# Five units' u times B: turned u scaled by columns of turned B on ScalarE, in place of products with diagonal matrices read back from DRAM

## What is computed

```python
dbc = jnp.einsum('bld,ed->ble', xi, x_proj)
dt, Bm, Cm = jnp.split(dbc, [DT_RANK, DT_RANK + D_STATE], axis=-1)
dt = jax.nn.softplus(jnp.einsum('blr,dr->bld', dt, dt_w) + dt_b)
A = -jnp.exp(A_log)
dA = jnp.exp(dt[..., None] * A)
dBx = (dt * xi)[..., None] * Bm[:, :, None, :]
def step(h, inp):
    a, bx, c = inp
    h = a * h + bx
    return (h, jnp.einsum('bds,bs->bd', h, c))
```

## Time and profile before

| | us |
|---|---|
| median of 3 runs | 4762.65 (4761.55 to 4768.12) |
| span of the profiled execution | 4760.7 |
| PE busy | 4479.5 (94%) |
| DVE busy | 3894.2 (82%) |
| ACT busy | 3109.7 (65%) |
| POOL busy | 3320.9 (70%) |

### The profile page before, as it was taken

How to read it: one execution, slowest core, us unless ns; L and a number is a source line. 1 busy time by engine, 2 the same in 40 slices (tenths; PEclk the granted TensorE clock), 3 DMA queues, 4 the chain that set the end, 5 groups by cost and what they waited for, 6 DMA issues and landing times. The chain is left out here.

```text
span 4760.7 us, 67108 instructions
## 1 busy us (share of the span) xinstructions
PE 4479.5 (94%) x24932; PEld 3395.1 (71%) x24932; DVE 3894.2 (82%) x4126; ACT 3109.7 (65%) x5158; POOL 3320.9 (70%) x1559
## 2 busy tenths in 40 slices
PE   7999999999999989999999999998799999999999
PEld 3666666666666666667666667666688888888888
DVE  5999999999999999999999999999854444444452
ACT  6777777777777777777777777777444444444443
POOL 4999999999999999999999999999820000000000
PEclk9999999999999999999999999999999999999999
DMA  7544444444444444444444444444231111010100
GB/s 271 178 142 141 134 151 132 136 134 134 143 139 134 155 132 138 129 139 139 131 147 140 129 130 136 143 142 156 103 123 32 36 32 36 32 36 32 36 23 10
DMA packets 297736, 545.76 MB, mean 115 GB/s; under 512 B 101888, under 2 KB 186624, under 8 KB 262784
## 3 DMA queue, kind: packets, MB, share of 16 engines
q1 hardware_dynamic: 296512, 529.91, 35.6%
q10 hardware_dynamic: 896, 11.54, 0.7%
HBM read 502.77 MB, written 50.14 MB: 116 GB/s over the span
## 5 line engine op out<-in xcount | busy, mean ns | idle before, releaser
L1400 DVE TENSOR_TENSOR_SCAN m_h<-bank,m_state,m_dBx 128x512 f32<-128x512 f32 x1512 | 1841.2, 1265 | 35.0 <-ACT bank L1145 27.2
L868 PEld LDWEIGHTS bank<-ident,m_h 128*128 128x128 f32 x8192 | 980.9, 143 | 417.2 <-issue 345.8
L868 PE MATMUL bank<-ident,m_h 128*128 128x128 f32 x8192 | 1197.6, 276 | 12.9 <-DVE m_h L1408 12.8
L1283 POOL TENSOR_TENSOR m_dBx<-u,m_Bs 128x1024 f32<-128x1024 f32 x432 | 1016.4, 2377 | 0.4 <-DMA m_Bs<-b_dram 0.2
L1283 POOL TENSOR_TENSOR m_dBx<-m_u,m_Bs 128x1024 f32<-128x1024 f32 x432 | 1015.5, 2371 | 1.2 <-DMA m_Bs<-b_dram 1.0
L1294 POOL TENSOR_TENSOR m_h<-m_h,m_Cs 128x1024 f32<-128x1024 f32 x384 | 909.4, 2368 | 105.8 <-ACT m_state L1077 105.1
L1408 DVE TENSOR_TENSOR m_h<-m_h,bank 128x1024 f32<-128x1024 f32 x640 | 767.0, 1198 | 51.7 <-PE bank L850 51.4
L1145 ACT ACTIVATE bank<-m_dt,cols 128x512 f32<-128x512 f32 x864 | 584.8, 688 | 225.2 <-DVE m_h L1400 223.7
L1145 ACT ACTIVATE bank<-dt,cols 128x512 f32<-128x512 f32 x864 | 584.1, 688 | 193.6 <-DVE m_h L1400 191.6
L302 POOL TENSOR_TENSOR mvj<-mvj,norm_c 128x4 f32<-128x4 f32 x16 | 16.5, 1032 | 969.0 <-DVE mvj L263 969.0
L731 PE MATMUL bank<-hT,w_in 128*128 128x512 f32 x1024 | 547.4, 630 | 113.1 <-ACT hT L998 105.8
(11 more groups left out here) (177 smaller groups left out, 5847.1 us busy)
## 6 DMA issues: line engine op xcount, KB each, us to landing
m_Bs<-b_dram SPq DMA_DIRECT2D x256, 1024.0 KB, 6.3
m_Cs<-c_dram SPq DMA_DIRECT2D x384, 256.0 KB, 3.7
m_dg<-d_dram SPq DMA_DIRECT2D x160, 256.0 KB, 3.9
xx<-in_x SPq DMA_DIRECT2D x16, 512.0 KB, 4.9
xn_dram<-xx SPq DMA_DIRECT2D x16, 512.0 KB, 4.5
yb_dram<-m_ysb SPq DMA_DIRECT2D x16, 512.0 KB, 5.0
xx<-xn_dram SPq DMA_DIRECT2D x16, 512.0 KB, 3.8
x_dram<-m_ysb SPq DMA_DIRECT2D x16, 512.0 KB, 5.0
```

The costliest lines, as they stand in the source:

```text
L868: mm = pe.matmul(YB[b][:, o:o + P], h[:, k % NH, m, tok:tok + P], ident[:, :], start=(s == 0 and o == 0), stop=False, is_transpose=True, s ...
L1283: pool.tensor_tensor(dBx[:, dbx_ring(ch, k) % NDBX, :, :], u[ch.batch][:, m, :], Bs[:, k // BP % 2, k % BP, :].unsqueeze(1).broadcast_to(( ...
L1400: dve.tensor_tensor_scan(o, decays, share, initial, ALU.mult, ALU.add).then_inc(S["scan"], 1)
```

## The change

The diagonal matrices go, with `d_dram`, its zeroing, the four writes per chunk, the loads and their semaphores. In their place a tile `m_uB` (same size as the two buffers of `m_dg`) holds the turned u scaled for one unit: on ScalarE `scale_u` multiplies each of the four token tiles (128 tokens x 256 channels) of `m_uT` by column k % 16 of the turned B, a scale per partition. The four activations of unit k stand at steps 2k - 5, 2k - 4, 2k - 3 and 2k - 2, behind the decay of the step. The first one waits until both fills of the five-unit list's previous unit are done (`a_fill`), since there is one `m_uB`. TensorE then turns `m_uB` into the bank with the identity, in transpose mode. ScalarE's copies of dt, B, C and of the turned u lose their waits for the diagonals' writes and the last fills.

```diff
-A_FIRST, A_STEP, NA = 19, 3, 5
-A_UNITS = tuple(A_FIRST + A_STEP * i for i in range(NA))
+A_UNITS = (19, 22, 25, 28, 31)
+NA = len(A_UNITS)
 B_UNITS = tuple(k for k in range(NU) if k not in A_UNITS)
-NBU, NDG, DIAG = len(B_UNITS), 2, T + 1
+NBU = len(B_UNITS)
+AT_US = (-5, -4, -3, -2)
...
-        dg = sb("dg", [P, NDG, TS, P])
+        uB = sb("uB", [P, TS, HW])
...
-            def store_diagonals(ch):
-
-                wait_drained(sp, ch, J_B)
-                if ch.first():
-                    sp.sem_inc(S["go"], 1)
-                    sp.wait_ge(S["d_init"], 16 * BATCH * NA)
...
-                sp.dma_start(dg[:, n % NDG, :, :], d_dram[ch.batch, i, 0:P * T].rearrange("(p t c) -> p t c", t=TS, c=P)
-                             ).then_inc(d_in[n % NDG], 16)
...
                     if m == 0:
-                        if i == 0:
-                            wait_drained(pe, ch, J_UT[1])
-                        pe.wait_ge(d_in[n % NDG], 16 * (n // NDG) + 16)
+                        pe.wait_ge(S["u_scaled"], n + 1)
                     pe.wait_ge(S["scan"], tile - NDA + 1)
                     for s in range(TS):
-                        mm = pe.matmul(DA[tile % NDA][:, s * P:(s + 1) * P], uT[:, s, m * P:(m + 1) * P],
-                                       dg[:, n % NDG, s, :], start=True, stop=True)
+                        mm = pe.transpose(DA[tile % NDA][:, s * P:(s + 1) * P], uB[:, s, m * P:(m + 1) * P], ident[:, :])
                     mm.then_inc(S["a_fill"], 1)
...
-                    if not ch.first():
-                        act.sem_inc(S["go"], 1)
-                        act.wait_ge(S["d_st"], ch.at(64, 0))
...
+            def scale_u(ch, g):
+
+                for i, k in enumerate(A_UNITS):
+                    for t in range(TS):
+                        if g != 2 * k + AT_US[t]:
+                            continue
+                        n = ch.at(NA, i)
+                        if t == 0:
+                            if i == 0:
+                                wait_drained(act, ch, J_UT[0])
+                                act.sem_inc(S["go"], 1)
+                                wait_drained(act, ch, J_UT[1])
+                                act.sem_inc(S["go"], 1)
+                                wait_drained(act, ch, J_C)
+                                act.sem_inc(S["go"], 1)
+                            wait(act, S["a_fill"], 2 * n)
+                        ins = act.activation(uB[:, t, :], uT[:, t, :], ACT.Copy,
+                                             scale=Ct[:, ch.batch, t, k % DS:k % DS + 1])
+                        if t == TS - 1:
+                            ins.then_inc(S["u_scaled"], 1)
...
+                    scale_u(ch, k)
```

More of the change, by code:

```diff
@@ L186, in adaln_mamba_ffn @@
         J = Join(S, x1, base, jx, jy, xn2, gain, norm_c, stat2, mvj, mv2)
-        d_dram = nc.dram_tensor("d_dram", (BATCH, NA, P * DIAG), F32, kind="Internal").ap()
         c_dram = nc.dram_tensor("c_dram", (BATCH, DS, T), F32, kind="Internal").ap()
         mamba(nc, a, bank, ident, cols, mod, gain, norm_c, fcol, any_odd, passes, w1, w2, J, x_v, yb_v, yf_v, xn_v, b_dram,
-              c_dram, d_dram, w_raw, S)
+              c_dram, w_raw, S)
         ffn(nc, a, sem, sbuf, bank, ident, mod, gain, fcol, any_odd, w1, w2, hT2, ot, J, w_raw, S, x_v, xn_v, yb_v, yf_v, out_v)
@@ L199 @@
     "sp_exp", "sp_ln", "dt_done", "u_ready", "b_st", "b_in0", "b_in1", "c_in0", "c_in1", "da", "dbx", "scan", "save",
-    "c_fill", "d_zero", "d_init", "d_st", "d_in0", "d_in1", "a_fill", "weigh_d", "weigh_p", "turned", "skip", "y_turned", "y_evac",
+    "c_fill", "u_scaled", "a_fill", "weigh_d", "weigh_p", "turned", "skip", "y_turned", "y_evac",
     "y_out", "xn_in", "xn_out",
@@ L356, in mamba @@
 def mamba(nc, a, bank, ident, cols, mod, gain, norm_c, fcol, any_odd, passes, w1, w2, J, x_v, yb_v, yf_v, xn_v, b_dram,
-          c_dram, d_dram, w_raw, S):
+          c_dram, w_raw, S):
     FB, DA, CB, YB = bank[0:2], bank[2:5], bank[5], bank[6:8]
     fill, drain = [S[f"fill{i}"] for i in range(NFB)], [S[f"drain{i}"] for i in range(NFB)]
-    b_in, c_in, d_in = (S["b_in0"], S["b_in1"]), (S["c_in0"], S["c_in1"]), (S["d_in0"], S["d_in1"])
+    b_in, c_in = (S["b_in0"], S["b_in1"]), (S["c_in0"], S["c_in1"])
     PASS = ("b_", "f_")
@@ L588, in load_c @@
                              ).then_inc(c_in[i % 2], 16)
-            def load_d(ch, i):
-                n = ch.at(NA, i)
-                wait(sp, S["a_fill"], 2 * (n - NDG + 1))
-                if i == 0:
-                    sp.sem_inc(S["go"], 1)
-                    sp.wait_ge(S["d_st"], ch.at(64, 64))
-                sp.dma_start(dg[:, n % NDG, :, :], d_dram[ch.batch, i, 0:P * T].rearrange("(p t c) -> p t c", t=TS, c=P)
-                             ).then_inc(d_in[n % NDG], 16)
             def store_y(ch):
@@ L628, in prologue @@
                 sp.dma_start(fcol[:, :, :], a["ffn_cols"]).then_inc(S["lng_in"], 16)
[L629 to L633, removed]
                 for n in range(6, 10):
@@ L638, in prologue @@
                 store_b(ch)
-                store_diagonals(ch)
                 for j in range(2):
@@ L675, in body @@
                 load_c(ch, 1)
-                load_d(ch, 0)
-                load_d(ch, 1)
                 if has(ch, 2):
@@ L696, in body @@
                     store_b(ch.go(1))
-                load_d(ch, 2)
                 load_c(ch, 8)
                 load_c(ch, 9)
-                load_d(ch, 3)
                 load_b(ch, 7)
@@ L705, in body @@
                 load_c(ch, 11)
-                load_d(ch, 4)
                 if has(ch, 1):
-                    store_diagonals(ch.go(1))
                     load_b(ch.go(1), 0)
@@ L1151, in keep_uT @@
                         wait_filled(act, ch, J_UT[m])
-                        wait(act, S["a_fill"], ch.at(2 * NA, 0))
                         b = BANK[J_UT[m]]
@@ L1330, in prologue @@
                 pool.memset(norm_c[:, 2, :], -1.0).then_inc(S["const"], 1)
-                pool.memset(dg[:, 0, :, :], 0.0).then_inc(S["d_zero"], 1)
                 pool.wait_ge(S["const"], 4)
```

1 line of the change is left out of this document (removed).

## The result

The changed kernel takes 4803.4 us (median of 4 runs, 4800.67 to 4805.4), the kernel before 4762.98 in the runs beside it: ratio 1.0082, 95% interval 1.0067 to 1.0096. It is slower, 40 us by the medians, against +49 forecast. The profiled execution's span is 4798.9 us, 38.2 above that of before.

The account below looks back on a forecast made before the run. VectorE bounds the kernel, its feeders just early enough. Per chunk +1.76 + 0.15 − 0.46 = +1.45 us, over 31 chunks +45, clock +4, on span 4760.7 gives 4810, median 4812 us; range 4764 to 4850.

Parts of the forecast that it names:

- The scaling's price: ScalarE's 20 new activations per chunk: 0.50 us each, 0.40 us of ACT time after overlap (0.28 to 0.49).
- The wait at step 51: ScalarE's step-51 scaling waits for unit 25's second fill, which waits for scan 48; the table load comes 1.22 us later.
- R3: Rival: the wait at step 51 does not bite, only the scalings' work; net 1.03 us a chunk, 4795 + 4; chance 0.13.
- DVE's stop: Late decays stop VectorE 1.56 us at scan 53, 1.76 us in all by scan 57, per chunk.
- Steps 33 to 37: Scalings at steps 33 and 34 delay ScalarE's copy of dt, B, C; VectorE's weighing comes 0.15 us later per chunk.
- Step 45: Shorter TensorE fills remove VectorE's wait for the spreading of C: −0.46 us a chunk (bounds nothing to −1.66).
- The clock: TensorE half-clock stretches at chunk starts, some 1.2 us each; four more chunks with one: +4 us.
- R1: Rival: TensorE's clock falls once more in every chunk, 37 in place of 4 us: 4845 us; chance 0.17.
- DMAs: Loads and writes of diagonals and the prologue's zeroing go; no engine waits for them: 0 taken, prologue 7 us at most.
- R2: Rival: TensorE is the real limit, shorter fills remove all waits for spreading (−51 us): 4712 to about 4740 us; chance 0.11.
- R4: Rival: VectorE's stop is given back as waits at the chunk's start shrink; 0.25 us a chunk, 4770 us; chance 0.09.

Follow-up runs that it names:

- The run with two buffers: The change with a second buffer for the scaled u of units 22 and 28, so no scaling waits for the previous unit's fills: 4770.1 us, ratio 1.0028.
- the filler: Unread identity transposes, 20 per chunk at step 1, added to the kernel with moved scalings: 4697.5 us; as ten identity products instead: 4698.6 us.
- the kernel before with filler: The kernel before the change plus 20 unread identity transposes per chunk on TensorE at step 1: 4723.8 us, ratio 0.9927.
- the moved kernel: The change with three buffers and its scalings moved to steps 34 to 46 and 58 to 60: 4728.4 us, ratio 0.9937.
- the +57 beside heavy fills: The kernel before with only the 20 scalings per chunk added, into a tile nobody reads, fills left as products with diagonals: 4816.1 us, ratio 1.0122.
- with filler, which takes step 5's wait away: The changed kernel plus twenty identity transposes by TensorE at the start of each chunk: 4775.0 us, ratio 1.0030.

## Why the prediction was right

The forecast was +1.45 us per chunk in 31 chunks, 4 for the clock and 2 from span to median. From the traces: chunk 31 begins 38.9 us later than before, and the first scan 2.3 us earlier, so 31 chunks grew by 41.2, 1.33 each (28 of them by 1.27, and 5.7 in all in chunks 0, 15 and 16, where a pass begins or ends); the last chunk is 3.7 shorter, and what follows it 2.9 longer. Step by step:

- *The scaling's price.* 0.50 us forecast, 0.501 measured; start to start 0.40 forecast, 0.399 measured (median), except ahead of the table load. Right.
- *The wait at step 51.* The table load was to come 1.22 us late by the wait and then ACT another 0.40. It comes 2.54 us after scan 48's start in place of 1.15, so 1.39 late; 0.17 more than forecast. The larger part of that is the scaling itself: the table load did not overlap it, so it took 0.52 us (1542.74 to 1543.26) and not 0.40; the rest is the fill, which takes 0.66 and not 0.60. The run with two buffers takes this wait out and gets 26 to 33 us back. Right, and shown. R3, that only the work bites (4795 to 4799 us), is wrong by this: without the wait the kernel takes 4770.
- *DVE's stop.* 1.56 at scan 53 and 1.76 in all forecast. Measured 1.59 at scans 52 and 53 together and 2.09 with scan 57, less the 0.20 that stood at steps 56 and 57: 1.9. From start to start it is 1.92, and that is what the slacks give with the measured 1.39 in place of 1.22 (1.39 + 3 x 0.40 − 0.66 = 1.93). Half of the stop already sits at scan 52, which I had not worked out.
- *Steps 33 to 37.* 0.15 forecast, 0.29 measured as idle time, 0.35 from start to start: undersized by half. ACT's idle time at step 46 did take up the lateness from before it: nothing is late at steps 39 to 48.
- *Step 45.* −0.46 forecast, −0.52 measured as idle time, −0.72 from start to start. The right place, undersized. In my list of what would show it I had DVE's waits for the spreading down by some 14 us; they fell by 7.6, because step 37's new wait is one of the same kind (+9.1); step 45's fell by 13.9, step 5's by 1.5 over all chunks, the last chunk's by 1.2.
- *The lighter fills in the last chunk.* Not in the sum: −3.7 us. TensorE's granted clock there is 0.95 in place of 0.90. All kernels with lighter fills have a last chunk of 102.1 to 103.8 us, those with heavy ones 105.4 to 108.3. How much of it is the clock isn't shown.
- *The clock.* +4 forecast. Half-clock stretches in chunks 1 to 30 are 24 with 116.0 us in all, before 26 with 109.2. By step 5's wait it cost −0.8 us a chunk in the first pass and +0.45 in the second, some −5 us in the 28 chunks; chunks 15 and 16, which had no such wait, now have one of 1.6 us each, so −1.5 in all. Of the 14 chunks of the first pass all had a wait at step 5 and now 4 have, of the second 6 had and now 9. The forecast had the wrong sign here. Nothing like R1's one more in every chunk. The rule of the Trainium skill (TensorE: Matmul & The Clock Gate, Part 4: PE-mode transpose) that transposes don't count as busy in the way that products do found no support in two pairs: the fills as transposes or as products (116.0 us of half clock both), and the filler (54.6 and 51.2 us).
- *DMAs.* 0 forecast, 0 measured (4728.6 against 4728.9). The first scan's 2.3 us are not the zeroing that went: the kernel before with filler, which keeps it, has its first scan at 78.9 us, the moved kernel, which does without, at 80.7.

R2, that TensorE is the real limit, has its true part: the lighter fill by itself is worth 30 us (4728.9), between my 14 (0.46 x 31) and the bound of 51. But it doesn't help past step 51: the fill of step 49 waits for scan 48 with PE idle ahead of it, as forecast. From kernel to kernel it is −30 for the fill (4728.9 against 4758.7), +41 for the scalings' work (4770.1 − 4728.9), +26 to 33 for the wait of step 51. That these come out at the +40 measured proves nothing, as each step starts where the one before ended. The independent price of the work is the +57 beside heavy fills, and with it the sum would be 53 to 60: the parts are not independent. Some 12 of the 16 us between lie in DVE's stops (1.95 us a chunk more beside heavy fills, 1.55 beside light ones); the rest is at the chunk's start, where the clock changes. R4, that the stop is given back at the chunk's start, is wrong too: with filler, which takes step 5's wait away, the stop is the same and the kernel still 0.3% slower than before.

The closeness of the total, 4812 against 4803.4, is in part luck, as errors of some 25 us one way and 13 the other stand in it. By the spans it is 4810 against 4799. Too high were the clock (some 10 us in the 28 chunks, from +4 to −0.20 a chunk), step 45 (7), the last chunk (3.7), the first scan (2.3) and small changes in other steps (2); too low were the stop and step 37 (0.16 and 0.20 us a chunk, 10 us) and what follows the last chunk (2.9). What stays open is why step 5's wait fell in the first pass and rose in the second: no run varied the stretch of TensorE's work ahead of a chunk's end.

## What to carry to other kernels

- Work added to an engine that is idle a quarter of the time costs nothing or everything, by its place: the same 640 activations cost 0 us at steps 34 to 46 and 58 to 60, and 69 to 75 us at steps that lie before a table load and behind a wait for another engine (41 the work, 26 to 33 the wait). Find the stretch in which the engine's rows follow each other without a hole, and keep new work and above all new waits out of it.
- A single buffer between two engines makes the producer wait for what the consumer waits for: here ScalarE waited for TensorE's fill, and the fill for VectorE's scan. A second one, from a tile that is free at that time, was worth some 30 us here.
- Where the clock of TensorE often falls after a wait, some useless work in the wait can be the cheapest gain in the kernel: 20 transposes a chunk gave 28 to 33 us in three kernels.
- A stop of an engine costs more than its idle time, 0.08 us here for each operation that starts from a wait. Starts of the operations, compared between two traces, show the full price.

## What the runs showed of the hardware

A 128x128 product of f32 operands is two pieces in the trace and a transpose one, each 0.28 us long with starts 0.11 us apart at full clock: a fill of four is 1.05 to 1.16 us as products and 0.60 to 0.66 as transposes. In the 28 chunks of the kernels before and after, the sizes of DVE's wait at step 5 (0, 0.9 to 1.4, 2.5 and 3.8 us) go with the length of the half-clock stretch that makes it, and a wait of TensorE of the same 2.72 us was followed by half clock in one chunk and by full clock in another. The half-clock stretches of chunks 1 to 30 do not go by TensorE's work: 109.2 us with the heavy fills of the kernel before, and 139.9 with lighter fills alone, 126.2 with moved scalings, 116.0 with the change and 102.3 with two buffers, all of which have the lighter fills. With lighter fills alone, DVE's wait at step 5 rose from 1.15 to 1.38 us a chunk and took back part of the gain; what makes the stretches more or fewer isn't shown.
